# Reading three copies of a part of k with one DMA whose source repeats its rows (layers 0 to 2 of a four-layer transformer kernel)

## What is computed

```
qkv = h @ w_qkv + b_qkv                     # q, k, v: (B, 16, 128, 9)
attn = softmax(einsum('bhqd,bhkd->bhqk', q, k) * 9 ** -0.5)
o = einsum('bhqk,bhkd->bhqd', attn, v)
```

## Time and profile before

| | |
|---|---|
| median of 3 runs | 1609.39 us (1606.48 to 1611.66) |
| the profiled execution | 1606.2 us, its span 1604.4 us |
| TensorE busy | 1451.3 us, 90% of the span |
| VectorE, ScalarE, GpSimd busy | 1045.6, 790.9, 541.6 us |
| granted clock of TensorE, mean | 0.959 |
| DMA queue of SP and ScalarE: 16 engines' time | 36.9% |
| attention of layer 0, 1, 2, 3 | about 52 to 250, 590 to 785, 900 to 1140, 1249 to 1508 us |

### The profile page before, as it was taken

How to read it: one execution, slowest core, us unless ns; L and a number is a source line. 1 busy time by engine, 2 the same in 40 slices (tenths; PEclk the granted TensorE clock), 3 DMA queues, 4 the chain that set the end, 5 groups by cost and what they waited for, 6 DMA issues and landing times. The chain is left out here.

```text
span 1604.4 us, 41580 instructions
## 1 busy us (share of the span) xinstructions
PE 1451.3 (90%) x15976; PEld 1063.3 (66%) x15976; DVE 1045.6 (65%) x2594; ACT 790.9 (49%) x1415; POOL 541.6 (34%) x739
## 2 busy tenths in 40 slices
PE   6789989999999998999998688877999799988998
PEld 2366676777777776666777466656676576666776
DVE  4688875666767667787447788896445465655342
ACT  2366664333323326666545366664554355555543
POOL 3345532211131304453334224433325234332321
PEclk9799999999999999999999889988999799999999
DMA  4765641111032214554011433453217676775021
GB/s 129 154 143 138 143 100 51 49 42 42 35 79 57 59 43 103 125 135 114 17 30 48 108 84 90 108 118 76 43 31 99 95 103 108 127 123 93 14 64 45
DMA packets 210861, 134.98 MB, mean 84 GB/s; under 512 B 144189, under 2 KB 193048, under 8 KB 204458
## 3 DMA queue, kind: packets, MB, share of 16 engines
q1 hardware_dynamic: 190706, 129.75, 36.9%
q10 hardware_dynamic: 19960, 2.57, 1.2%
HBM read 98.24 MB, written 33.24 MB: 82 GB/s over the span
## 5 line engine op out<-in xcount | busy, mean ns | idle before, releaser
L1212 ACT ACTIVATE prob<-banks 128x1024 f32<-128x1024 f32 x256 | 262.2, 1024 | 216.3 <-PE banks L669 215.4
L1520 DVE TENSOR_REDUCE negm<-banks 128x8 bf16<-128x1024 f32 x256 | 311.3, 1216 | 80.7 <-PE banks L647 77.8
L1939 POOL TENSOR_TENSOR X<-X,gx 128x288 f32<-128x288 f32 x128 | 104.2, 827 | 288.0 <-DVE gx L1550 285.8
L1338 ACT ACTIVATE hid<-banks 128x512 f32<-128x512 f32 x144 | 85.9, 597 | 229.5 <-PE banks L945 229.4
L647 PE MATMUL banks<-qk 54*128 54x128 bf16 (+1 forms) x2048 | 124.1, 244 | 70.5 <-DVE negm L1520 38.9
L665 PE MATMUL banks<-qk 54*128 54x128 bf16 (+1 forms) x2048 | 170.9, 238 | 10.1 <-ACT prob L1212 7.2
L960 PEld LDWEIGHTS banks<-wfc,hid 128*128 128x128 f32 x1152 | 157.5, 191 | 30.0 <-issue 20.1
L680 PE MATMUL banks<-prob,V 128*32 128x128 f32 x4096 | 173.5, 289 | 2.5 <-ACT OT L1218 2.4
L669 PE MATMUL banks<-mT,pick 64*128 64x128 bf16 x2048 | 167.6, 227 | 0.0
L960 PE MATMUL banks<-wfc,hid 128*128 128x144 f32 x1152 | 162.1, 287 | 0.0
L944 PE MATMUL banks<-hT,wfc 128*128 128x512 f32 x288 | 149.1, 599 | 1.1 <-DMA wfc<-in_L_cond_w 0.6
(11 more groups left out here) (166 smaller groups left out, 2818.8 us busy)
## 6 DMA issues: line engine op xcount, KB each, us to landing
qk<-qk_scr SPq DMA_DIRECT2D x336, 72.0 KB
gbuf<-gate_scr SPq DMA_DIRECT2D x64, 288.0 KB, 4.4
qk_scr<-parts SPq DMA_DIRECT2D x48, 288.0 KB, 3.0
qk<-qk_scr SPq DMA_DIRECT2D x48, 216.0 KB
qk<-cw_scr SPq DMA_DIRECT2D x8, 1024.0 KB, 4.7
qk<-tok_scr SPq DMA_DIRECT2D x112, 72.0 KB
qk_scr<-parts SPq DMA_DIRECT2D x48, 144.0 KB, 2.5
qk<-qk_scr SPq DMA_DIRECT2D x48, 144.0 KB
```

Source lines behind the costliest of these rows:

```text
L1212: act.activation(prob[:, 2 * (U % 2):2 * (U % 2) + 2, :], pairs[1][:], ACT.Exp, scale=scale).then_inc(a_exp, 1)
L1520: dve.tensor_reduce(negm[:, u // 2, :, 4 * (u % 2):4 * (u % 2) + 4], pairs[0][:].rearrange("q s (h k) -> q s h k", k=T), AX.X, ALU.max, ne ...
L1939: pool.tensor_tensor(x, x, gx[:, q, :, :], ALU.add).then_inc(g_x, 1)
```

## The change

In layers 0 to 2 the k rows of a part are read by one DMA. Its destination is all 27 (or 18) partitions of the part, its source is the 9 rows with a leading dimension of step 0 and size 3 (or 2). So a group has 6 DMAs a side, 12 in all, in place of 18; `fetched` counts 96 a group for groups below 24. Layer 3 is as before. What bytes arrive where is unchanged.

```
         def fetched(n):
-            return 144 * (n // 3 + 1)
+            i = n // 3 + 1
+            return 96 * i if n < 24 else 96 * 8 + 144 * (i - 8)
...
                         sp.dma_start(q_dst, q_src[0:rows]).then_inc(q_r[r][s], 16)
-                        for i in range(3 - part):
-                            sp.dma_start(k_dst[D * i:D * i + D], k_src[D * part:D * part + D]).then_inc(q_r[r][s], 16)
+                        k_new = k_src[D * part:D * part + D]
+                        if l < 3:
+                            if part < 2:
+                                k_new = k_new.unsqueeze(0).to_broadcast([3 - part] + list(k_new.shape))
+                            sp.dma_start(k_dst, k_new).then_inc(q_r[r][s], 16)
+                        else:
+                            for i in range(3 - part):
+                                sp.dma_start(k_dst[D * i:D * i + D], k_new).then_inc(q_r[r][s], 16)
                         r0 += rows
```

## The result

| | before | changed |
|---|---|---|
| median | 1610.53 us (4 runs, 1606.48 to 1619.2) | 1709.45 us (4 runs, 1705.45 to 1713.58) |
| ratio | | 1.0595 (95% interval 1.0558 to 1.0633) |
| span of the profiled execution | 1604.4 us | 1709.5 us |
| mean granted clock of TensorE | 0.959 | 0.923 |

The changed kernel is 6.0% slower, 99 us by the medians. The forecast had the sign, but +24 us, and the time lies above its range.

A forecast was written before the change was run, and what follows sets the result against it. TensorE, busy 90%, waited 14.2 us for reads, which nine DMA engines set. Layers 0 and 1 +18 us, layer 2 +6, last groups +3, slack -3: +24 us, about 1633 us median; range 1610 to 1700.

The forecast's parts named there:

- Engines: Group reads, layers 0 to 2: repeated sources use three and two engines; the two busiest carry 50 rows instead of 24.
- Price of the rows: On the busiest engines: about 12 rows at 0.45 us, then 38 at 0.33, 17.9 us in all.
- +2.0 us per group: Reads of a group, first issue to use: 19.3 us against 17.3.
- What of it reaches the end: Layers 0 to 2: a delay counts half, giving 18 us in layers 0 and 1, 6 us in layer 2.
- What queues behind: Next group's writes land later on the two busy engines: 1.0 us a group in layers 0 and 1, nothing in layer 2.
- which wait for the start anyway: Layer 0's first two groups, said to be the exception to first reads having time to spare during the MLP before.
- The 1 us for the last group of a layer: Last group of each of three layers has no next one to hide half the delay: 3 x 1 = 3 us.
- The MLPs and layer 3 keep their length: Sign that the forecast is right: outside the attention of layers 0 to 2, no stretch gets longer.
- Issues: SP issues 12 DMAs in place of 18, 2.1 us less of its time per group, priced at nothing.
- (a): Rival: rows in the reads stay dear, 0.45 to 0.61 us each, adding 80 to 190 us; chance 0.14.
- (b): Rival: repeated source spreads over nine engines, reads take 11 us, TensorE's 14.2 us come back, 1595 us; chance 0.07.

The follow-up runs named there:

- by dimension: Kernel before with the 54 rows ordered by dimension, copies innermost, so sources' outermost size is 9: 0.9959 with twelve joined transfers, 0.9973 with eighteen.

## Why the prediction was wrong

The number of engines was right. The price of the rows was not; nor was the share of a delay that reaches the end in layer 2, and two terms were missing, the start and the clock. The forecast said +24 us, measured were 99.

*Engines.* Right. A source that repeats 3 or 2 times in its outermost dimension went over three and two engines; the share fell to 0.15 (2.4 engines), and putting the repeat inside took all of the loss away.

*Price of the rows.* The term "+2.0 us per group" failed; it measured +4.7. I had "about 12 rows at 0.45 us, as long as the other seven engines are still at work". That phase took 8.8 us by the medians, where 5.4 were allowed; the later rows took 11.9 (36 at 0.33), where 12.5 were. The six lightly loaded engines have 14 rows, and as long as they work, nine engines pay about 0.6 us a row with the gaps, as before; concentration does not make these rows cheaper. The cheap rows were priced well (0.33 us, and that is the mean of the packets that began after the first phase). The upper phase's price stood in the third of the earlier trace rows. With prices near it (fitted afterwards): 14 x 0.58 + 18 x 0.37 + 18 x 0.32 + 1.4 = 21.9 us.

*What of it reaches the end.* "So a delay counts half" was said of reads and queue together. So taken it held in layer 0 (3.8 us by the rule, 3.7 measured) and nearly in layer 1 (2.8 and 3.4); in layer 2 it failed (2.4 by the rule, 5.3 measured). I had used the order of layers 0 and 1 for layer 2, though two of its three products of q and k stand past the wait; the front of this document has them in units 2 to 4. With the measured sizes of reads and queue the rule gives 54 us for the 18 groups, and 71 with layer 2's 5.3 us; the rest of the 105 us of the traces lies at the start, around the MLPs and in layer 3.

*What queues behind.* "I add 1.0 us" was too little in layer 0 (+2.9 us for the last write to land), right in layer 1 (+0.9): the reads and the weights were still under way on the loaded engines when the writes were issued. "Layer 2, nothing" was right (2.7 us in both).

*The first groups.* I priced the reads of groups 0 and 1 at nothing, "which wait for the start anyway". By the landing of group 2 the changed kernel was already 12.9 us behind, about 9 of it from these two. The 1 us for the last group of a layer was too little as well: between the landings of groups 7 and 10, with layer 0's MLP between, another 13.2 us were lost, 6.2 of them TensorE's longer work.

*The clock.* It stood in no term, and "The MLPs and layer 3 keep their length" failed with it. TensorE's busy time grew by 42.4 us at a granted clock of 0.923 in place of 0.959, in every stretch of the table above. Where TensorE is busy nearly throughout, as from the landing of group 23 to the end, this goes straight into the time (8.1 us more busy, 5.4 us longer). In the loops it overlaps with the waits, and no run measured its share of the 99 us alone.

*Issues.* Priced at nothing, rightly, but for the wrong reason: "2.1 us less of SP's time" was not there to be hidden. 12 issues take the time of 18.

Of the rivals, (a) came nearest in time (80 us at 0.45 us a row and nearly full passage), yet its mechanism is not what happened: the last rows are cheap. (b) fell by the share. The gain from joining transfers of which it speaks did not show either: joined over nine engines, the reads take 17.1 us, unjoined 17.4. What did make the kernel faster was in no rival: the order of issue to the two halves.

## What to carry to other kernels

Before you join DMAs by repeating the source, look at the outermost size: put the size that gives many engines (here the 9 rows) outside and the repeat inside. Price a transfer that is concentrated on few engines in phases, each at the price of the engines then at work, and ask what is queued behind it on those engines. Where reads land just as they are needed, extra time can cost much more than the same saving gives. Find, layer by layer, which work of the next round stands before the wait and which behind it, before you take a fraction; and when the busiest engine is made to wait more often, look at its granted clock, since the same work may then take longer. When transfers go to two halves of the partitions, try issuing them in turn.

## What the runs showed of the hardware that I had not expected

- The order of issue of 18 transfers to two halves of the partitions was worth 1.4% of the kernel, layer 3 included. In layers 0 to 2: rows from 0.61 to 0.49 us, reads from 17.4 to 14.4 us, with the same nine engines.
- A transfer from SP with a third dimension or a stepped destination takes longer to issue: 0.76 and 0.63 us for 27 and 18 rows with a repeated source, 0.7 to 0.8 us by dimension, 12.4 us for 18 transfers with destinations 3 or 2 partitions apart, against 0.35 us and 6.4 us.
- TensorE took 1493.7 us for the instructions that took 1451.3 us before, at a mean granted clock of 0.923 in place of 0.959, in a run where its waits for reads grew by 71.7 us.
- Nine engines reading one and the same 8 KB row over and over were slower (0.67 us) than reading different rows (0.61 us); a pitch of 15 in place of 16 KB changed nothing.
